# Spreading fp32 transposes between the 512-column products on TensorE

## The reference

```python
x = x + _L0_conv_ref(_gn(x))                  # 192x192 piece of a scaled 256x256 Hadamard matrix, per pixel
x = x + _L1_conv_ref(_gn(x), W1, b1, g1, beta1, W2, b2, g2, beta2, W3, b3)

# _gn: group norm, 32 groups of 6 channels over all pixels of an image
# _L1_conv_ref, on the 192 channels of each pixel:
h = h @ W1.T + b1;  h = gelu(layernorm(h, g1, beta1), approximate=False)
h = h @ W2.T + b2;  h = gelu(layernorm(h, g2, beta2), approximate=False)
h = h @ W3.T + b3
```

## Time and profile before

| | |
|---|---|
| median of three runs | 927.61 us |
| span of the profiled execution | 927.5 us |
| PE busy | 831.8 us (90%) |
| ACT busy | 814.3 us (88%) |
| DVE busy | 799.5 us (86%) |
| POOL busy | 551.2 us (59%) |
| transposes to bank 0 (L590) | 784, 278 ns each |
| chain that ended last | PE 48%, DVE 31%, ACT 10%, POOL 7% |

### The profile page before, as it was taken

One profiled execution on the slowest core, in us unless ns is written; L12 is line 12 of the kernel. 1 busy time (PEld: TensorE's weight loads), 2 busy tenths in 40 slices (PEclk: granted clock), 3 DMA queues, 4 the chain that ended last, 5 costly groups with the idle time before them and its releaser, 6 DMA issues.

```text
span 927.5 us, 22221 instructions
## 1 busy us (share of the span) xinstructions
PE 831.8 (90%) x8353; PEld 552.3 (60%) x8353; DVE 799.5 (86%) x1416; ACT 814.3 (88%) x2400; POOL 551.2 (59%) x414
## 2 busy tenths in 40 slices
PE   0646889899999999999999999999999999889897
PEld 0114545556666666666666666666666667566663
DVE  6699898999999999999999999999998887745455
ACT  0687879689999999999999999999999998999982
POOL 0452544566666666666666666766766666577760
PEclk9987999999999999999999999999999999999999
DMA  9725022223323333233233232332111113121213
GB/s 265 234 69 145 1 70 69 74 69 104 107 69 108 103 105 98 81 103 108 70 110 101 94 117 70 98 113 84 59 40 55 50 36 104 40 69 35 70 36 102
DMA packets 52090, 81.99 MB, mean 88 GB/s; under 512 B 14608, under 2 KB 14736, under 8 KB 51856
## 3 DMA queue, kind: packets, MB, share of 16 engines
q1 hardware_dynamic: 51984, 80.58, 28.8%
HBM read 41.23 MB, written 39.32 MB: 87 GB/s over the span
## 4 chain that ended last, share of the span: by engine, by line
PE 48%; DVE 31%; ACT 10%; POOL 7%; issue 2%; SPq 1%; DMA 1%; ACTq 0%; DVEq 0%; POOLq 0%
PE tm L578 11%; DVE z L1248 6%; PE tm L573 5%; PE tp L590 5%; DVE X L1089 5%; DVE xs_lo L1080 4%; POOL ge_lo L943 4%; PE hl L487 4%; DVE bn L1106 3%; DVE x_lo L1230 3%; PE hl L418 3%; ACT z L729 3%; PE tm L567 3%; PE hl L516 2%; PE hl L492 2%; PE hl L511 2%
## 5 line engine op out<-in xcount | busy, mean ns | idle before, releaser
L943 POOL TENSOR_TENSOR ge_lo<-ge,ge_hi 128x512 f16<-128x512 f32 (+1 forms) x190 | 314.1, 1664 | 189.7 <-ACT ge_hi L759 189.7
L729 ACT ACTIVATE z<-tm 128x194 f32<-128x194 f32 x784 | 250.8, 346 | 41.9 <-PE tm L578 38.6
L935 POOL TENSOR_TENSOR rs<-ssq,neg_half 128x4 f32<-128x4 f32 x196 | 204.9, 1046 | 124.1 <-ACT z L729 123.2
L1248 DVE TENSOR_TENSOR z<-tm,rs 128x768 f32<-128x768 f32 x196 | 186.0, 949 | 62.1 <-POOL rs L935 61.3
L729 ACT ACTIVATION_READ_ACCUMULATOR z<-tm 128x1 f32 x784 | 175.1, 223 | 0.0
L741 ACT ACTIVATE ge<-tp,par 128x512 f32<-128x512 f32 x196 | 155.2, 792 | 21.1 <-PE tp L590 20.5
L759 ACT ACTIVATE ge_hi<-ge 128x512 f16<-128x512 f32 (+1 forms) x190 | 161.8, 855 | 2.9
L1089 DVE SCALAR_TENSOR_TENSOR X<-hl,h_bias,X 128x512 f32<-128x512 f32 x138 | 102.0, 741 | 30.6 <-PE hl L423 30.1
L590 PE MATMUL tp<-cst,z 128*128 128x128 f32 x784 | 121.8, 278 | 4.9 <-DVE z L1248 2.8
L1230 DVE SCALAR_TENSOR_TENSOR x_lo<-X,gscale,x_hi 128x512 f16<-128x512 f32 x144 | 102.8, 743 | 1.1 <-ACT x_hi L706 1.1
L590 PEld LDWEIGHTS tp<-cst,z 128*128 128x128 f32 x784 | 85.7, 142 | 28.4 <-issue 21.7
(11 more groups left out here) (192 smaller groups left out, 1888.2 us busy)
## 6 DMA issues: line engine op xcount, KB each, us to landing
out<-X SPq DMA_DIRECT2D x48, 512.0 KB, 2.9
X<-x SPq DMA_DIRECT2D x40, 512.0 KB, 4.0
out<-X SPq DMA_DIRECT2D x98, 128.0 KB, 3.0
X<-x SPq DMA_DIRECT2D x80, 128.0 KB, 4.1
X<-x SPq DMA_DIRECT2D x8, 576.0 KB, 4.2
X<-x SPq DMA_DIRECT2D x16, 144.0 KB, 4.4
X<-weights SPq DMA_DIRECT2D x1, 1024.0 KB, 12.1
out<-X SPq DMA_DIRECT2D x8, 64.0 KB, 3.0
```

Of the source, the lines that this page charges most:

```text
L729: last = nc.scalar.activation(z[n][:, 2 * h + k, i * TW:(i + 1) * TW], tm[h][:, i, k * TW:(k + 1) * TW], ACT.Square, scale=float(C) ** -0. ...
L935: nc.gpsimd.tensor_tensor(rs[n][:, 2 * h:2 * h + 2, :], ssq[n][:, 2 * h:2 * h + 2, :], neg_half[0:TT, 0:4].rearrange("p (i k) -> p i k", i=2),
L943: nc.gpsimd.tensor_tensor(ge_lo[n][:, g % 2, PART[h], :], ge[n][:, PART[h], :], ge_hi[n][:, g % 2, PART[h], :], ALU.subtract).then_inc(s_g ...
L1248: nc.vector.tensor_tensor(z[n][:, 2 * h:2 * h + 2, 0:2 * C].rearrange("p k (i o) -> p i k o", i=2), tm[h][:, :, 0:2 * TW].rearrange("p i ( ...
```

## The change

It touches PE's queue alone. Three runs of six transposes are handed as extra arguments to the function of the product that follows them. That function issues its own waits and its first product, then a transpose, then the next product, and so on. `h_ab` places four transposes behind its first four products and two after those; `l3_ab` places six behind its six; `l3_c` places two behind each of its three. The fourth run of a pass, `transposes(g - 1, 1, 0)`, stays as it was. In `last` the two of layer 3 are treated in the same way; `first` and `drain` are not changed. No instruction is added or removed.

```diff
-            def h_ab(a):
+            def h_ab(a, *turned):
                 if not 0 <= a < N:
+                    if turned:
+                        transposes(*turned)
                     return
                 pe.wait_ge(s_xs_lo, a + 1)
                 free("a", "b")
...
                         nc.tensor.matmul(hl[:, i, 0:UT], h16[:, AA, :], part[:, i, :], start=(r == 0), stop=False,
                                          skip_group_check=True)
+                        if turned:
+                            transpose(*turned, 2 * i + r)
+                if turned:
+                    transposes(*turned, 4)
...
-            def l3_ab(g):
+            def l3_ab(g, *turned):
...
+                        if turned:
+                            transpose(*turned, 3 * i + r)
...
-            def l3_c(g):
+            def l3_c(g, *turned):
...
+                    if turned:
+                        transpose(*turned, 2 * r)
+                        transpose(*turned, 2 * r + 1)
...
-            def transposes(g, n, h):
+            def transpose(g, n, h, j):
                 if not 0 <= g < NL:
                     return
-                pe.wait_ge(s_z[n], 2 * g + h + 1)
-                done = 3 * g + h
-                free("tp0")
...
+                if j == 0:
+                    pe.wait_ge(s_z[n], 2 * g + h + 1)
+                    free("tp0")
+                if j < 4:
+                    k, i = divmod(j, 2)
...
+                    if j == 3:
+                        last.then_inc(s_tp[n], 1)
+                        held["tp0"] = s_ge[n], 3 * g + h + 1
+                    return
...
+            def transposes(g, n, h, first=0):
+                for j in range(first, 6):
+                    transpose(g, n, h, j)
...
             def step(g):
                 group(g, 0, 0)
-                transposes(g - 2, 1, 1)
-                h_ab(h_unit(g, 0))
+                h_ab(h_unit(g, 0), g - 2, 1, 1)
                 group(g, 0, 1)
...
                 h_left(h_unit(g, 0))
-                transposes(g, 0, 0)
-                l3_ab(g - 2)
+                l3_ab(g - 2, g, 0, 0)
                 group(g - 1, 1, 1)
-                transposes(g, 0, 1)
                 w1_shift(gn2_pair(g))
                 h_shift(h_shift_pair(g))
-                l3_c(g - 2)
+                l3_c(g - 2, g, 0, 1)
                 transposes(g - 1, 1, 0)
```

More of the change, by code:

```diff
@@ L580, in group @@
                     last.then_inc(s_mm[n], 1)
-            def transposes(g, n, h):
+            def transpose(g, n, h, j):
                 if not 0 <= g < NL:
                     return
-                pe.wait_ge(s_z[n], 2 * g + h + 1)
-                done = 3 * g + h
-                free("tp0")
[L588 to L594, removed]
+                if j == 0:
[3 more added lines that the diff above has]
+                    k, i = divmod(j, 2)
+                    at = (0, C + CC)[i]
+                    last = nc.tensor.transpose(tp[:, 0, i * HALF + k * TT:i * HALF + (k + 1) * TT],
+                                               z[n][:, 2 * h + k, at:at + 128], ident[0:TT, 0:TT])
+                    if j == 3:
+                        last.then_inc(s_tp[n], 1)
+                        held["tp0"] = s_ge[n], 3 * g + h + 1
+                    return
+                k = j - 4
+                if k == 0 and h == 0:
                     free("tp1")
[L596 to L599, removed]
+                last = nc.tensor.transpose(tp[:, 1, h * HALF + k * TT:h * HALF + (k + 1) * TT], z[n][:, 2 * h + k, CA:CA + 128],
+                                           ident[0:TT, 0:TT])
+                if k == 1 and h == 1:
                     last.then_inc(s_tp[n], 1)
-                    held["tp1"] = s_ge[n], done + 2
+                    held["tp1"] = s_ge[n], 3 * g + 3
+            def transposes(g, n, h, first=0):
+                for j in range(first, 6):
+                    transpose(g, n, h, j)
             def first(g):
```

## The result

The changed kernel takes 976.15 us (median of four runs, 973.66 to 976.77) against 927.45 us for the kernel before on the same chip (four runs): ratio 1.0512, 95% interval 1.0493 to 1.0532. It is slower by 48.7 us; the prediction had 37 (965). It reached pass 6 3.8 us earlier than that of before did.

What follows compares the result with a forecast made beforehand. The prediction took PE to be the bound by a small margin, with ACT and DVE close behind. 927.5 + 36.2 for 36 passes + 1 for `last` gave 964.7, predicted as 965 us, range 944 to 975.

Steps and rivals of the forecast that it cites:

- Bound and interleaving at 0: PE's own work bounds a 15.86 us pass; moved transposes still take 0.109 us each, so interleaving itself costs 0.
- the rival of the weight loads: fp32 weight loads set the transposes' pace; behind a product each costs 0.055 us, not 0.109: 940 us, chance 0.07.
- Bare wait ahead of `l3_c`: Layer 3's block 2: transposes no longer cover PE's wait for `final_ab`; 0.60 us lost in each plain pass.
- the rival that had nothing else: Only the covers of waits are lost, ACT catches up: 36 passes cost 19 us, 947 us, chance 0.2.
- Later GELU: Fourth transposes come later, GELUs start 0.54 to 0.60 us late; with the bare wait, 1.07 us per plain pass.
- second term: The later GELU's delay through `x_hi`: DVE gets it 0.46 us late at `x_lo`, so `final_ab` ends late.
- Other passes: Passes unlike the plain one: 0.6 us off where DVE is late, 1.7 with `h_left`, 0.65 added with `w1_shift`.
- the credit of 0.6: One pass where DVE itself takes `h_ab` late hides up to 0.8 us of inherited delay; 0.6 taken off.
- `last`: In its six passes the transposes of `l3_c` come 0.44 us later; the chain loses 0.1 to 0.2 each: +1.
- Sum: Six passes cost 6.03 us, the 36 of `step` 36.2; with 1 for `last`, 964.7, predicted as 965 us.
- the rival at 979: ACT becomes the bound through idle time ahead of three GELUs; a plain pass costs 1.5 us: 979 us, chance 0.12.

Runs made afterwards that it cites:

- `l3_c` alone: Changed kernel with the transposes of `h_ab` and `l3_ab` back in runs of six, only those of `l3_c` interleaved: 955.0 us, 1.0275 of the kernel before.
- the moved kernels: On DVE, one `x_lo` moved behind `final_ab`, or the first `xs_lo` moved earlier; from the kernel before 949.4 and 994.23 us, from the changed one 996.47 and 1034.76.
- `l3_ab` alone: Changed kernel with the transposes of `h_ab` and `l3_c` back in runs of six, only those of `l3_ab` interleaved: 947.6 us, 1.0203 of the kernel before.

## Why the prediction was right or wrong

- **Bound and interleaving at 0.** Right. Pairs stand at 0.22 and 0.11, the clock stayed 1.00 in this stage, and the rival of the weight loads is refuted (by it a pair would take 0.275).
- **Bare wait ahead of `l3_c`.** Right: 0.94 us in the pass shown, in the forecast's 0.6 to 1.1. The kernel with only the waits moved puts the share of lost covers at 23.9 us, near the 19 of the rival that had nothing else; in a plain pass the cover's share is about 0.63 for 0.60.
- **Later GELU.** Right that it makes the other part. The sum for a plain pass came out near (1.23 and 1.08 grown for a forecast of 1.07), but that is partly luck, for the route was another. The prediction let 0.46 enter by `x_hi` and `x_lo`, and named as the sign of a wrong second term that DVE never waits at `x_lo`. In the plain passes `x_lo` did not wait. ACT, POOL and DVE:

```profile
520.69 0.78 ACT L764 ACTIVATE ge<-tp,par 128x512 f32<-128x512 f32 x1
...
522.65 1.05 ACT L782 ACTIVATE ge_hi<-ge 128x1024 f16<-128x1024 f32 x1
...
532.62 0.78 ACT L764 ACTIVATE ge<-tp,par 128x512 f32<-128x512 f32 x1 [0.77 <-PE tp L612]
```

```profile
523.77 2.14 POOL L966 TENSOR_TENSOR ge_lo<-ge,ge_hi 128x1024 f16<-128x1024 f32 x1 [1.41 <-ACT ge_hi L782]
```

```profile
521.46 0.75 DVE L1112 SCALAR_TENSOR_TENSOR X<-hl,h_bias,X 128x512 f32<-128x512 f32 x1 [0.76 <-PE hl L430]
522.39 0.96 DVE L1271 TENSOR_TENSOR z<-tm,rs 128x768 f32<-128x768 f32 x1 [0.19 <-POOL rs L958]
...
524.53 0.73 DVE L1112 SCALAR_TENSOR_TENSOR X<-hl,h_bias,X 128x512 f32<-128x512 f32 x1
...
525.78 1.39 DVE L1103 SCALAR_TENSOR_TENSOR xs_lo<-X,gscale,xs_hi 128x512 f16<-128x512 f32 x2
527.41 0.96 DVE L1271 TENSOR_TENSOR z<-tm,rs 128x768 f32<-128x768 f32 x1 [0.24 <-POOL rs L958]
...
528.94 1.41 DVE L1253 SCALAR_TENSOR_TENSOR x_lo<-X,gscale,x_hi 128x512 f16<-128x512 f32 x2
530.27 1.21 DVE L1302 SCALAR_TENSOR_TENSOR X<-hl,X 128x1024 f32<-128x1024 f32 x1
```

  DVE before, the two `normalise` of the same stretch (`residual` at 501.81 is in the earlier trace rows):

```profile
502.47 0.95 DVE L1248 TENSOR_TENSOR z<-tm,rs 128x768 f32<-128x768 f32 x1
...
507.16 0.95 DVE L1248 TENSOR_TENSOR z<-tm,rs 128x768 f32<-128x768 f32 x1
```

  DVE's stretch grew by 0.60 at two places. From `residual` to the first `normalise` it is 0.93 us instead of 0.66. This comes from `l3_c`: ACT waits 0.77 for its fourth transpose (532.62 is the same moment one pass later), `ge_hi` and `ge_lo` follow late, `rs` stands behind `ge_lo` in POOL's queue, and `normalise` waits for `rs`. The kernel with `l3_c` alone has the same 0.18 of wait. The prediction let this delay fall into ACT's and gave it nothing. From the first `normalise` to the second it is 5.02 instead of 4.69. This comes from `h_ab`: `ge_lo` ends 0.54 later behind `residual` than before (525.91 - 521.46 = 4.45 for 3.91), as forecast, and `rs` behind it now starts inside `xs_lo` and lasts 1.51 (row at 525.87 above). With 1.01 it would end at 526.88, ahead of `xs_lo` at 527.17, and nothing would wait. So these 0.33 us come from the exclusion that the moved kernels showed, not from the length of the chain. This is read from rows; no kernel isolates it. The prediction saw that `ge_lo` moves, but asked only PE about it, not what is queued behind it on POOL. The route by `x_lo` is the one of `l3_ab` alone (0.26 of wait in a plain pass there) and, in the changed kernel, of the pass with `h_left`, as forecast: 1.54 of wait, for 1.6.

```profile
600.71 1.42 DVE L1253 SCALAR_TENSOR_TENSOR x_lo<-X,gscale,x_hi 128x512 f16<-128x512 f32 x2 [1.54 <-ACT x_hi L729]
```

- **The step that failed in size: "Other passes".** 1.72 us are missing in six passes. The largest piece is the credit of 0.6 for DVE being late itself in the pass with the statistics: "up to 0.8 of the delay that the pass before brings is hidden there". The third pass of the table holds 1.07 - 0.6 = 0.47 of the forecast and grew by 1.27. The credit would be due if the delay came to DVE from PE. But it sits in DVE's own queue, which is full from `final_ab` to the residual and hands it on whole: from `l3_ab` to this residual it was 550.33 - 538.72 = 11.61 us, and is 572.87 - 560.15 = 12.72.

```profile
572.87 0.75 DVE L1112 SCALAR_TENSOR_TENSOR X<-hl,h_bias,X 128x512 f32<-128x512 f32 x1
```

  Next comes the pass with `w1_shift`, 1.14 for 0.65: the transposes now behind the wait were counted, not that the wait itself grows (1.19 for the 0.53 of the earlier trace rows), `final_ab` being late by the same GELUs. The two passes between grew by 3.03 for 2.77. With the old order in these last three alone, 3.45 of their 4.17 went; that the third stayed at 18.66 fits a delay that is handed on.
- **`last`.** Five of its passes are 0.2 longer each, near the forecast, the sixth 0.8: 1.7 for the 1 of the forecast.
- **Sum.** 36.2 forecast for `step`, 46.4 measured, with 1.7 for `last` and 3.8 less ahead of `step`: 44.3 between the profiled executions, while the medians differ by 48.7. The two causes, lost cover and late GELUs, were right, one of the routes was not; the price is 11 us too low, and the time lies 1.15 us above the range. ACT did not become the bound (45.01 busy of 50 us), so the rival at 979 is nearest in time but not in cause.

## What to carry to other kernels

Work that stands in a queue just ahead of a wait is a cover; moved behind the wait, it costs as much of the wait as it hid, here up to its whole 0.65 us, in each place where a wait stands, the rare ones too. Ask of each result in a moved run when its last consumer wants it, and follow each delay along the whole queue of every engine that it reaches. A delay can also push two instructions onto one another that used to miss each other. If transposes must be spread, spread those whose reader comes last: with four of six left in place the loss fell from 48.7 to 7.9 us, and no version was faster than the kernel before.

## What the runs showed of the hardware

- VectorE with two SBUF tensors as inputs and GpSimd with two exclude one another for whole instructions: 0.74 us became 1.38 and 2.34 in the rows shown, and moving one instruction in DVE's queue cost 20 to 64 us. A queue tuned by hand can hold such a rule unwritten.
- A GpSimd instruction of 128x4 grew from 1.01 to 1.5 us beside such a VectorE instruction, also where the profile has it start 0.04 us ahead of it.
- fp32 transposes of 128 columns cost the array 0.11 us beside a 512-column product, with their weight load already over, as in a row; those of 64 tokens, in a row, 0.06 each behind the first.
- Less work on TensorE went with less clock: with shorter transposes PE was busy 31.69 of 38 us instead of 34.83 from 850 to 888 us, at a mean granted clock of 0.91 instead of 1.00.
